# Value matmuls over two tiles at once: scores of two tiles in a row, then the pair's values

## The reference

```python
xn = layernorm(x, ln1_w, ln1_b)          # x: the context, (16, 1444, 128)
ln = layernorm(latents, ln2_w, ln2_b)    # latents: the tokens, (16, 100, 128)
q = ln @ Wq
kv = xn @ Wkv
...
qk = jnp.einsum('bihd,bjhd->bhij', q, k) * attn_scale      # 16 heads of 64
attn = jax.nn.softmax(qk, axis=-1)
out = jnp.einsum('bhij,bjhd->bihd', attn, v)
return out.reshape(b, -1, INNER) @ Wout
```

## Time and profile before

| what | us |
|---|---|
| median of 3 runs | 1341.62 |
| profiled execution, its own time | 1341.98 |
| its span, first to last instruction | 1340.2 |
| PE busy | 1156.0 (86%) |
| VectorE busy | 1152.7 (86%) |
| ScalarE busy | 876.6 (65%) |
| GpSimd busy | 620.2 (46%) |

### The profile page before, as it was taken

How to read it: one execution, slowest core, us unless ns; L and a number is a source line. 1 busy time by engine, 2 the same in 40 slices (tenths; PEclk the granted TensorE clock), 3 DMA queues, 4 the chain that set the end, 5 groups by cost and what they waited for, 6 DMA issues and landing times. The chain is left out here.

```text
span 1340.2 us, 32623 instructions
## 1 busy us (share of the span) xinstructions
PE 1156.0 (86%) x12753; PEld 900.3 (67%) x12758; DVE 1152.7 (86%) x2860; ACT 876.6 (65%) x1202; POOL 620.2 (46%) x512
## 2 busy tenths in 40 slices
PE   3576999999999999999999999999995639777778
PEld 2463677777777767776777777777674628677668
DVE  5796899999999999999999999998884288999984
ACT  0246888889888888888888888888872632222121
POOL 2344667566675667757577575775220000000000
PEclk9768999999999999999999999999997766666666
DMA  7007999999999999999999999999997000000000
GB/s 156 1 6 139 191 191 187 203 200 190 200 192 201 193 194 196 199 198 198 193 200 198 195 199 193 184 184 173 189 193 162 11 0 2 5 5 6 5 5 6
DMA packets 671121, 185.78 MB, mean 139 GB/s; under 512 B 655828, under 2 KB 668536, under 8 KB 670840
## 3 DMA queue, kind: packets, MB, share of 16 engines
q1 hardware_dynamic: 670968, 183.71, 80.3%
HBM read 19.51 MB, written 0.82 MB: 15 GB/s over the span
## 5 line engine op out<-in xcount | busy, mean ns | idle before, releaser
L1046 PE MATMUL ps<-pT,xa_hi 128*128 128x128 f16 x2288 | 381.1, 217 | 17.5 <-DMA pT<-p 16.7
L851 ACT ACTIVATE e<-ps,bias 128x1444 f32<-128x1444 f32 (+1 forms) x208 | 305.7, 1470 | 132.6 <-DVE bias L923 132.0
L1042 PE MATMUL ps<-pT,xa_hi 128*128 128x128 f16 x2288 | 382.8, 217 | 8.5 <-ACT uT L874 8.2
L1043 PE MATMUL ps<-pT,xa_lo 128*128 128x128 f16 x2288 | 382.8, 217 | 0.0
L921 DVE TENSOR_REDUCE nmax<-ps 128x1 f32<-128x1444 f32 (+1 forms) x208 | 343.9, 1653 | 19.3 <-PE ps L1026 18.6
L933 DVE TENSOR_TENSOR p<-e,p 128x1408 f16<-128x1408 f32 (+3 forms) x288 | 303.9, 1096 | 35.6 <-ACT p L859 34.5
L859 ACT ACTIVATE p<-e 128x1408 f16<-128x1408 f32 (+1 forms) x208 | 288.2, 1386 | 13.3
L811 POOL TENSOR_TENSOR p<-e,p 128x1408 f16<-128x1408 f32 (+1 forms) x128 | 196.6, 1556 | 182.9 <-ACT p L859 182.9
L1042 PEld LDWEIGHTS ps<-pT,xa_hi 128*128 128x128 f16 x2288 | 222.1, 98 | 33.6 <-issue 19.1
L1046 PEld LDWEIGHTS ps<-pT,xa_hi 128*128 128x128 f16 x2288 | 222.0, 98 | 24.2 <-DMA pT<-p 24.0
L1024 PE MATMUL ps<-xT_hi,q_hi 128*128 128x512 f16 (+1 forms) x624 | 229.9, 368 | 8.0 <-DMA xT_lo<-xa_lo 7.4
(11 more groups left out here) (225 smaller groups left out, 1910.4 us busy)
## 6 DMA issues: line engine op xcount, KB each, us to landing
raw<-in_ctx SPq DMA_DIRECT2D x16, 704.0 KB
pT<-p SPq DMA_TRANSPOSE x416, 4.2
f_wq<-in_L_ffn_w_q SPq DMA_DIRECT2D x1, 1024.0 KB, 4.9
f_wqt<-in_ffn_wq_t SPq DMA_DIRECT2D x2, 512.0 KB, 7.0
raw<-in_ctx SPq DMA_DIRECT2D x48, 18.0 KB
x_tok<-in_x SPq DMA_DIRECT2D x1, 800.0 KB
out_x<-ost SPq DMA_DIRECT2D x6, 128.0 KB, 2.0
wk_t<-in_wk_t SPq DMA_DIRECT2D x1, 512.0 KB, 5.7
```

Source lines behind the costliest of these rows:

```text
L851: act.activation(e32[t % E_BUF][rows, :], score_banks(t)[rows, 0:T], ACT.Exp, bias=bias[rows, t % N_BUF:t % N_BUF + 1]).then_inc(e_done, 1)
L1042: pe.matmul(out, hi, ph, start=n == 0, stop=False)
L1043: pe.matmul(out, lo, ph, start=False, stop=False)
L1046: pe.matmul(out, hi, pl, start=False, stop=False)
```

## The change

PE does the value matmuls of tiles 0 and 1, 2 and 3, ..., 10 and 11 of a batch together, in matmuls of 256 columns; tile 12 stays by itself. `values(t)` is called at the second tile of a pair alone (`pair_end`), at the same place of the loop as that tile's values before, and waits for both tiles' halves: for the high halves at its start, for the low halves ahead of the third matmul. The number of value matmuls falls from 13 x 34 to 7 x 34 per batch. `pT` holds 4 pairs in place of 6 tiles, with the two tiles' columns of one block of keys side by side, so that a tile's blocks are 256 columns apart. A transposing DMA waits until the values of the pair four pairs earlier are done (`tiles_through`). `pv_done` counts tiles as before, two at a time. The order on the other engines and their instructions stay as they were.

```diff
--- before.py
+++ after.py
@@ -608,7 +608,9 @@
 
 
 LAG = 4
-RING = 6
+RING = 8
+PAIRS = (NM + 1) // 2
+PAIR_RING = 4
 E_BUF, P_BUF, N_BUF = 2, 3, 4
 LAST = HQ - (NM - 1) * P
 GT = 4
@@ -672,6 +674,21 @@
     return sum(j[0] == JOBS[k][0] for j in JOBS[:k + 1])
 
 
+def pair_number(t):
+
+    return t // NM * PAIRS + t % NM // 2
+
+
+def pair_end(t):
+
+    return t % NM % 2 == 1 or t % NM == NM - 1
+
+
+def tiles_through(q):
+
+    return q // PAIRS * NM + min(2 * (q % PAIRS) + 2, NM)
+
+
 def group_end(t):
 
     return t % NM % GT == GT - 1 or t % NM == NM - 1
@@ -707,7 +724,7 @@
         nmax, bias = sb("nmax", [P, N_BUF]), sb("bias", [P, N_BUF])
         e32 = [sb(f"e32_{i}", [P, T]) for i in range(E_BUF)]
         p = [sb(f"p{i}", [P, PB * P], F16) for i in range(P_BUF)]
-        pT = sb("pT", [P, RING, PB, P], F16)
+        pT = sb("pT", [P, PAIR_RING, PB, 2, P], F16)
         uT = sb("uT", [D, HQ])
         ry = sb("ry", [S, H])
         acc = sb("acc", [S, D])
@@ -735,8 +752,9 @@
 
         def value_bank(t):
 
-            cols, at = tile_cols(t % NM), t % NM % GT * P
-            return ps[:, 6, at:at + cols.stop - cols.start]
+            first, last = tile_cols(t % NM // 2 * 2), tile_cols(t % NM)
+            at = first.start % (GT * P)
+            return ps[:, 6, at:at + last.stop - first.start]
 
         job_bank = ps[:, 7, :]
 
@@ -753,16 +771,16 @@
             def turn_high(t):
                 rows = tile_rows(t % NM)
                 sp.wait_ge(hi_done, t + 1)
-                if t >= RING:
-                    sp.wait_ge(pv_done, t - RING + 1)
-                sp.dma_start_transpose(pT[:, t % RING, 0:TF, 0:rows.stop - rows.start],
+                if pair_number(t) >= PAIR_RING:
+                    sp.wait_ge(pv_done, tiles_through(pair_number(t) - PAIR_RING))
+                sp.dma_start_transpose(pT[:, pair_number(t) % PAIR_RING, 0:TF, t % NM % 2, 0:rows.stop - rows.start],
                                        p[t % P_BUF][rows, 0:TF * P]).then_inc(pT_hi_ld[t % RING], 16)
 
             def turn_low(t):
                 rows = tile_rows(t % NM)
                 sp.wait_ge(lo_pool if t % NM in POOL_LO else lo_dve, lo_of(t))
                 sp.wait_ge(again_hi, t + 1)
-                sp.dma_start_transpose(pT[:, t % RING, TF:PB, 0:rows.stop - rows.start],
+                sp.dma_start_transpose(pT[:, pair_number(t) % PAIR_RING, TF:PB, t % NM % 2, 0:rows.stop - rows.start],
                                        p[t % P_BUF][rows, TF * P:PB * P]).then_inc(pT_lo_ld[t % RING], 16)
 
             sp.wait_ge(xh_done, 1)
@@ -1029,29 +1047,33 @@
             def values(t):
 
                 b, i = divmod(t, NM)
-                pe.wait_ge(pT_hi_ld[t % RING], 16 * (t // RING + 1))
-                if i % GT == 0 and t:
+                tiles = range(t - i % 2, t + 1)
+                for k in tiles:
+                    pe.wait_ge(pT_hi_ld[k % RING], 16 * (k // RING + 1))
+                if i // 2 * 2 % GT == 0 and tiles[0]:
                     pe.wait_ge(u_done, group_number(t))
+                if i == 1:
+                    pe.wait_ge(cx.xa_mix_done, b + 1)
                 out = value_bank(t)
-                w = tile_cols(i).stop - tile_cols(i).start
-                if i == 0:
-                    pe.wait_ge(cx.xa_mix_done, b + 1)
+                w = tile_cols(i).stop - tile_cols(tiles[0] % NM).start
+                turned = pT[:, pair_number(t) % PAIR_RING, :, :, :].rearrange("k n a q -> k n (a q)")
                 for n in range(TF):
                     hi, lo = xa_hi[b % 2][:, n, :], xa_lo[b % 2][:, n, :]
-                    ph, pl = pT[:, t % RING, n, 0:w], pT[:, t % RING, TF + 1 + n, 0:w]
+                    ph, pl = turned[:, n, 0:w], turned[:, TF + 1 + n, 0:w]
                     pe.matmul(out, hi, ph, start=n == 0, stop=False)
                     pe.matmul(out, lo, ph, start=False, stop=False)
                     if n == 0:
-                        pe.wait_ge(pT_lo_ld[t % RING], 16 * (t // RING + 1))
+                        for k in tiles:
+                            pe.wait_ge(pT_lo_ld[k % RING], 16 * (k // RING + 1))
                     pe.matmul(out, hi, pl, start=False, stop=False)
-                last = pe.matmul(out, xa_mix[b % 2][:, :], pT[:, t % RING, TF, 0:w], start=False, stop=True)
-                last.then_inc(pv_done, 1)
+                last = pe.matmul(out, xa_mix[b % 2][:, :], turned[:, TF, 0:w], start=False, stop=True)
+                last.then_inc(pv_done, len(tiles))
 
             job("q", 0, 0)
             for t in range(ALL_TILES + DRAIN):
                 if t < ALL_TILES:
                     scores(t)
-                if 0 <= t - LAG < ALL_TILES:
+                if 0 <= t - LAG < ALL_TILES and pair_end(t - LAG):
                     values(t - LAG)
                 for j in jobs_of(t):
                     job(*j)
```

## The result

The changed kernel takes 1389.31 us (median of 4 runs, 1375.84 to 1395.23), the kernel before beside it 1342.78 (1341.55 to 1344.81): a ratio of 1.033, 95% interval 1.025 to 1.041. The direction was forecast, the size was not: +46.5 us instead of +14. The profiled execution took 1392.41 us, 50.4 more than that of before.

The account below looks back on a forecast made before the run. It took a VectorE and ScalarE loop as the bound, PE a nearly late feeder. 15 passages x 0.9 = 13.5 us, plus 0.8 in the last batch, made 14.3 on 1341.98: forecast 1356 us, range 1336 to 1382.

Parts of the forecast that it names:

- PE is not the bound: Whole kernel: PE is a feeder that is nearly late, with 0 to about 1.3 us of slack per batch passage.
- no gain from its saved work: PE: 8.4 us of matmul time saved, worth nothing by itself; the rival with PE as bound said 1333, chance 0.12.
- A 256-query matmul takes 109 ns: PE's value matmuls: 109 ns taken for 256 columns, between 108 and 111.6, against 55.8 for 128.
- The transfers are not slower: Transposing DMAs: a rival had the non-contiguous layout cost 30%, some 1490 us, chance 0.04.
- uT(7) follows V(6,7) at once: ScalarE's copy of tile 7's value group starts right after the pair's value matmuls, no longer behind the queries.
- Four of the pairs are free: Pairs other than 6, 7, these four among them: covered by slack, so cost zero.
- the sentence on the other pairs: All pairs but 6, 7: zero cost; at V(0,1) a head job stands behind, but uT(12) has long been copied.
- the third rival: Pairs stall in several places, such as a late V(0,1) delaying the head job ahead of max(6): 1382 us, chance 0.14.
- Its sign: VectorE's max(6) or max(1) late by a PE job would show the rival of stalls in several places.
- The term for V(6,7): Batch passage: waiting for low(7), these values end 1.70 us later; after slack 0.9 us, times 15 passages, 13.5 us.
- S(12): Tile 12's scores stand behind the pair 6, 7: max(12) late by about as much as uT(7), not counted twice.
- The fall: Clock falling in PE's new idle time: same 1382 us and more; longest earlier wait 1.3 us, clock at 1.00.

Follow-up runs that it names:

- the five wide pairs without the loss: Changed kernel with GpSimd's xa_lo ahead of the small power, q_lo of place 6 behind low(7), and tiles 6 and 7 single in 128-query matmuls: 1341.8 us.
- the kernel with GpSimd's two operations moved: Changed kernel with GpSimd's xa_lo ahead of the small power at place 5 and q_lo of place 6 behind low(7): 1348.05 us.
- the kernel with this pair alone: Kernel before with only the values of tiles 6 and 7 issued in a row, as 128-query matmuls: 1356.45 us.
- the pair 0, 1 alone: Kernel before with only the values of tiles 0 and 1 issued in a row, as 128-query matmuls: 1373.84 us.
- the kernel without the wait at place 10: Kernel before with values of tiles 6 and 7 in a row and query jobs at places 1, 2, 6, 9 instead of 1, 6, 9, 10: 1359.33 us.
- the one with the head job first: Changed kernel with the previous batch's last head job issued at place 5 ahead of V(0,1) instead of behind it: 1361.6 us.
- all six pairs in order: Kernel before with the values of all six pairs issued in a row at the pair's end, still as 128-query matmuls: 1388.01 us.
- three kernels that changed the order alone: Kernel before with 128-query values in a row for tiles 0, 1 (1373.84 us), tiles 6, 7 (1356.45), or the other four pairs (1343.53).

## Why the prediction was wrong

What held: PE is not the bound, and no gain from its saved work shows (the five wide pairs without the loss are no faster than single tiles). A 256-query matmul takes 109 ns. The transfers are not slower. uT(7) follows V(6,7) at once. Four of the pairs are free.

The step that failed is the sentence on the other pairs, "Cost of all this: zero, with the covers named", at V(0,1). It found the head job behind the pair and asked whether uT was waiting for it. It did not ask VectorE, in whose queue that job stands ahead of max(6); the third rival did, and named 1382 us with a chance of 0.14, but priced the delay itself. Its sign came, max(6) late by a PE job. But the delay is not the price: the kernel with GpSimd's two operations moved has the same delay and not the loss. The price is that VectorE's and GpSimd's operations, which passed each other by 0.4 us or less in the kernel before, now meet. In the profiled execution of after the middle 13 batches pay, from rows: 13 x 1836 ns less 13 x 173 = 21.6 us on L558; 13 x (0.55 on low(6) + 0.40 on xa_lo) = 12.4; 13 x 0.43 for the pair 6, 7 = 5.6; 3 x some 1.7 for the clock = 5.1. That is 44.7 us, and with the 2 us of the two batches in which PE waits for low(7) 46.7, where these batches grew by 46.0. Some 4 of the 50.4 us lie in the first and last batches and behind them, and were not followed up. The mean that this uses:

```profile
L558 DVE TENSOR_SCALAR cve<-cmv 128x12 f32<-128x12 f32 x13 | 23.9, 1836 | 0.4
```

The reading that was missed stood in the prediction's own rows: "low(5) is started at 535.37 and takes 3.77 us", while low(6), the same shape, takes 1.73. The number was used as a time of arrival; why it was twice as long was not asked. The 2.48 us of low(1) are such a sign too. None of the prediction's timelines is GpSimd's. The Trainium skill has the mechanism, in "SBUF — State Buffer", Who interferes with whom: VectorE and GpSimd share a pair of ports, a VectorE operation with two inputs in SBUF contends with a GpSimd operation that reads SBUF, one in a two-port mode with any, and whoever starts first holds the ports to its end. The trace agrees where low(5) waits out xa_lo, where low(6) and q_lo take turns, and where the addition begins 0.01 us behind low(7) and ends with it; in which mode the addition runs is in no row.

The term for V(6,7), 13.5 us, came out at 12.6, but its parts did not. It was to be 0.9 us in each batch through uT(7), because V(6,7) would wait for low(7) to land. It is 0.3 to 0.5 through S(12), which had been counted as late by about as much, and some 2.1 where the clock falls. V(6,7) waited for a landing in two of the 13 batches of the changed kernel and in none of the kernel with this pair alone. The fall was mentioned only under the third rival, and set against the longest wait of the value matmul, 1.3 us. The wait that came is another: PE at the query job, 2.03 us.

Open: why the clock falls in six of 13 batches, of which twelve hold this wait in full, and why not in the others. From the second batch to the fifteenth of all profiled executions it falls 14 times, always at or right behind a wait of PE of 2.0 to 2.7 us (nine times at the query job of place 10, five times, with the pair 0, 1 alone, at a head job), and never in a batch without such a wait; but 22 of these 36 long waits bring no fall. In the kernel without the wait at place 10 it fell in none, and in the one with the head job first, where PE waits 0.84 us at that job, in none either. That the wait brings it on is likely, not shown.

Why the addition meets low(7) in some batches and not in others, the traces show in part. By the timelines both follow from the late head job: the addition by way of max(6), q_lo and low(6), low(7) by way of the small power, xa_lo, low(5), max(7), exp(7) and high(7). So they start almost together. In each of the 39 middle batches of the three kernels whose L558 lengthens there (after, all six pairs in order, the pair 0, 1 alone) the profiled execution has them start within 14 ns of each other. Where GpSimd was first by 6 ns or more, 13 batches, the addition waited; where it was first by 5 ns or less, or second, 26 batches, it did not. Before, the addition was ahead by 0.54 us. What moves these few ns is open. In the plain eighth batch of the kernel with the pair 0, 1 alone, both begin at the same hundredth of a microsecond and the addition gets through in 0.17:

```profile
558.89 0.17 DVE L558 TENSOR_SCALAR cve<-cmv 128x12 f32<-128x12 f32 x1
```

```profile
558.89 3.10 POOL L812 TENSOR_TENSOR p<-e,p 128x1408 f16<-128x1408 f32 x2 [2.44 <-ACT p L860]
```

A race that is so close, at 2.7 us a batch, would explain that executions of the same kernel lie 20 us apart; how often it was lost in executions that were not profiled is inferred from that.

## What to carry to other kernels

An engine's "busy" holds waiting that no row of waits shows: compare durations of the same form in one batch, and where one is twice as long as its neighbour, look at what GpSimd does in the same microseconds. When a change shifts an engine in a periodic kernel, list not only who waits for it, but also which operations of VectorE and GpSimd pass each other closely, and what each meeting costs; a cover that is used up shows there. And price a change by its places one at a time: three kernels that changed the order alone gave 30, 12.6 and 0 us, where the whole gave one number that fitted several stories.

## What the runs showed of the hardware that was not expected

An addition of 128 x 12 numbers takes VectorE 0.17 us, and 2.87 to 2.89 when GpSimd has begun a subtraction just before it, by 6 ns or more. VectorE's subtractions and GpSimd's take turns, instruction by instruction: a low half that begins 0.9 us into xa_lo ends 1.6 us after it, and one of 1.73 us with a GpSimd subtraction of 0.94 that begins 0.42 us behind it take 2.48 and 2.01. The 128 x 1 addition for the bias (L941) and the maxima from PSUM never lengthened beside GpSimd (0.15 and 1.65 us).

GpSimd waits in the same way. In the middle stage of the kernel before, all 42 normalizations (L576, a tensor_scalar of 128 x 127) that begin while VectorE is at a large half take 1.8 to 2.2 us, the other 112 take 0.81 to 0.83. VectorE did not wait for them: 28 large halves began 0.47 to 0.71 us into a normalization, with no GpSimd subtraction near, and took 1.63 us as alone. By the Trainium skill's rule above VectorE would have waited for the end of that normalization; the trace does not show it, and no row tells whether the ports were free by then.
